# A decoder layer on one core: the rounding of the feed-forward rows moves from VectorE to ScalarE, and every engine's order is written anew

## The reference

```
x = layernorm(x + attention(x))        # width 256, 16 heads, windows of 128 positions
x = layernorm(x + ssm(ctx, z=x))       # state space: 512 channels, 16 states, 512 steps
x = layernorm(x + ffn(x))

def activation_quant(x):
    s = 127.0 / jnp.max(jnp.abs(x), axis=-1, keepdims=True)
    return jnp.clip(jnp.round(s * x), -128, 127) / s
xq = activation_quant(rms_norm(x))
g = jax.nn.silu(ternary_matmul(xq, W_g))
u = ternary_matmul(xq, W_u)
return ternary_matmul(g * u, W_d)      # the weights enter by their sign alone
```

## Time and profile before

| | |
|---|---|
| time, three runs | 989.22, 989.76 (median), 994.29 us |
| the profiled execution | 994.08 us, its span 992.4 us |
| mean TensorE clock granted in the span | 0.901 of full speed |
| busiest engines | DVE 865.3, PE 844.2, ACT 659.4, POOL 440.6 us |

### The profile page before, as it was taken

How to read it: one execution, slowest core, us unless ns; L and a number is a source line. 1 busy time by engine, 2 the same in 40 slices (tenths; PEclk the granted TensorE clock), 3 DMA queues, 4 the chain that set the end, 5 groups by cost and what they waited for, 6 DMA issues and landing times.

```text
span 992.4 us, 12690 instructions
## 1 busy us (share of the span) xinstructions
PE 844.2 (85%) x4258; PEld 532.1 (54%) x4258; DVE 865.3 (87%) x1200; ACT 659.4 (66%) x1115; POOL 440.6 (44%) x259
## 2 busy tenths in 40 slices
PE   1987887799978988999979889989978889876997
PEld 1446575585446565665446555665446565553453
DVE  0388999999799899999789999999789999999564
ACT  1586556566679586886687687886777687783332
POOL 2025755552335473542355564551365654554000
PEclk9997667769888889999998998999989999999899
DMA  7022323330100020100101121100000010000000
GB/s 221 31 77 76 106 96 129 95 97 11 44 11 33 22 75 22 37 18 12 44 12 33 33 75 29 36 11 12 23 13 31 33 41 25 32 13 11 11 12 32
DMA packets 29215, 43.92 MB, mean 44 GB/s; under 512 B 6128, under 2 KB 10096, under 8 KB 29152
## 3 DMA queue, kind: packets, MB, share of 16 engines
q1 hardware_dynamic: 25808, 41.74, 13.0%
q10 hardware_dynamic: 3344, 1.38, 0.6%
HBM read 38.78 MB, written 4.33 MB: 43 GB/s over the span
## 4 chain that ended last, share of the span: by engine, by line
DVE 45%; PE 29%; issue 15%; ACT 8%; POOL 2%; SPq 1%; DMA 1%; DVEq 0%; POOLq 0%; ACTq 0%
DVE h L1463 16%; DVE acc L1480 11%; PE bank_f L2355 3%; PE bank_a L2214 3%; PE bank_m L2331 3%; DVE s_pT L1348 2%; PE bank_f L2430 2%; DVE p_lo L1548 2%; ACT L896 2%; DVE g_p L1544 2%; DVE neg_max L1354 2%; PE bank_a L2259 2%; ACT d_a L861 2%; ACT L861 2%; PE bank_m L2297 2%
## 5 line engine op out<-in xcount | busy, mean ns | idle before, releaser
L514 POOL TENSOR_TENSOR b_x<-u,b_row 128x1024 f32<-128x1024 f32 x124 | 315.4, 2549 | 274.7 <-DVE h L1463 273.9
L1463 DVE TENSOR_TENSOR_SCAN h<-d_a,b_x 128x1024 f32<-128x1024 f32 x128 | 294.5, 2309 | 1.5 <-ACT d_a L861 1.5
L2331 PE MATMUL bank_m<-ident,h 128*128 128x128 f32 x1024 | 179.5, 309 | 51.6 <-DVE acc L1480 40.7
L861 ACT ACTIVATE d_a<-delta,a_neg 128x511 f32<-128x511 f32 x256 | 168.9, 712 | 33.1 <-DVE h L1463 32.7
L2331 PEld LDWEIGHTS bank_m<-ident,h 128*128 128x128 f32 x1024 | 134.6, 160 | 99.1 <-DVE h L1463 37.5
L1480 DVE SCALAR_TENSOR_TENSOR acc<-bank_m,c_cols,acc 128x512 f32<-128x512 f32 x256 | 185.8, 737 | 1.9 <-PE bank_m L2331 0.2
L896 ACT ACT_TABLE_LOAD x48 | 61.6, 1283 | 56.6 <-PE bank_f L2355 56.4
L791 ACT ACTIVATE s_pT<-s_pT,neg_max 128x128 f32<-128x128 f32 x256 | 81.4, 389 | 18.1 <-DVE neg_max L1354 18.0
L502 POOL TENSOR_TENSOR rs<-ve,neg_half 128x1 f32<-128x1 f32 (+1 forms) x36 | 36.3, 1009 | 120.1 <-DVE neg_mean L1565 69.0
L2241 PE MATMUL bank_a<-k_par,qT 32*128 32x256 f32 x256 | 79.6, 433 | 8.0 <-DVE s_pT L1348 6.1
L2259 PEld LDWEIGHTS bank_a<-v_aug,s_pT 128*128 128x128 f32 x512 | 70.8, 212 | 11.1 <-ACT s_pT L799 7.0
(11 more groups left out here) (180 smaller groups left out, 1476.7 us busy)
## 6 DMA issues: line engine op xcount, KB each, us to landing
b_row<-bc_rows SPq DMA_DIRECT2D x64, 256.0 KB, 3.1
x_next<-in_x_dram SPq DMA_DIRECT2D x4, 1024.0 KB, 5.5
y<-in_L_ffn_W_g_dram SPq DMA_DIRECT2D x16, 256.0 KB, 2.7
xn<-in_L_ffn_W_u_dram SPq DMA_DIRECT2D x16, 256.0 KB, 2.7
g_p<-in_L_ffn_W_d_dram SPq DMA_DIRECT2D x16, 256.0 KB, 3.0
out_dram<-y SPq DMA_DIRECT2D x16, 256.0 KB, 2.0
cx<-in_ctx_dram SPq DMA_DIRECT2D x4, 512.0 KB, 5.1
wc<-in_L_attn_Wc_dram SPq DMA_DIRECT2D x1, 512.0 KB, 10.0
```

The source lines that it names most:

```text
L514: nc.gpsimd.tensor_tensor(b_x[:, half], du[:, halves(half)], b_row[:, n % 2].unsqueeze(1).to_broadcast([P, EH, S]), ALU.mult)\
L861: last = nc.scalar.activation(d_a[:, half, c, 1:S], delta[:, half * EH + c, 1:S], ACT.Exp, scale=a_neg[:, half * EH + c, bass.ds(n, 1)])
L1463: nc.vector.tensor_tensor_scan(flat(h[:, (n + 1) % 2, halves(half)]), flat(d_a[:, half]), flat(b_x[:, half]), 0.0, ALU.mult, ALU.add).then ...
L2331: last = tr(bank_m[bank][:, c * P:(c + 1) * P], h[:, (n + 1) % 2, c, i * P:(i + 1) * P], ident[:])
```

## The change

1. `quantise` loses its last two instructions. ACT gets them as `round_rows`, two activations with the function Identity: the first adds `ROUND` (a column of the new tile `round_col`) to the row times `q_mul`, the second subtracts `ROUND` and writes 16 bits. PE's transposes wait for the new semaphore `xq_ready`.
2. The lower clip, which was part of the second rounding step, joins the upper one in DVE's copy of the transposes, in batches and in the tail.
3. The lists of all engines are written anew, in all their parts. `round_rows` is placed in ACT's lists.
4. In the tail `tail_product` waits for the transposes of two products before, since the buffer it writes is no longer covered by the order alone; and the second wait for the copied transposes is given to `tail_ups` too.

```diff
-Q_STEPS = 6
+Q_STEPS = 4
+        round_col = sb("round_col", [P, 2])
-        CONSTS = 10
+        CONSTS = 12
+            nc.gpsimd.memset(round_col[:, 0:1], ROUND).then_inc(consts_done, 1)
+            nc.gpsimd.memset(round_col[:, 1:2], -ROUND).then_inc(consts_done, 1)
...
+            def round_rows(n, t):
+
+                act.wait_ge(q_step, Q_STEPS * n + Q_STEPS)
+                nc.scalar.activation(xn[:], x2b[:, t], ACT.Identity, bias=round_col[:, 0:1], scale=q_mul[:, 0:1])\
+                    .then_inc(xn_ready, 1)
+                act.wait_ge(xn_ready, n + 1)
+                nc.scalar.activation(xq[:], xn[:], ACT.Identity, bias=round_col[:, 1:2]).then_inc(xq_ready, 1)
...
             def quantise(n, b, t):
...
-                dve.wait_ge(q_step, base + 4)
-                nc.vector.tensor_scalar(xn[:], rows, q_mul[:], ROUND, ALU.mult, ALU.add).then_inc(q_step, 1)
-                dve.wait_ge(q_step, base + 5)
-                nc.vector.tensor_scalar(xq[:], xn[:], -ROUND, Q_MIN, ALU.add, ALU.max).then_inc(q_step, 1)
             def quantised_T(n):
...
-                                        Q_MAX, None, ALU.min).then_inc(f_free[1], 1)
+                                        Q_MAX, Q_MIN, ALU.min, ALU.max).then_inc(f_free[1], 1)
...
             def tail_product(w, q):
                 k = NQ * w + q
+                if k >= 2:
+                    dve.wait_ge(tail_pT, k - 1)
...
             def quantised_T(n):
-                pe.wait_ge(q_step, Q_STEPS * n + Q_STEPS)
+                pe.wait_ge(xq_ready, n + 1)
...
-                quantise(row(b, w + 1), b - 1, w + 1)
...
+                quantise(row(b, w + 1), b - 1, w + 1)
                 low(row(b, w), 2)
```

1415 lines of the change are left out of this document (714 added, 701 removed).

## The result

The changed kernel takes 985.54 us (median of 7 runs, 983.44 to 986.33) against 991.8 us for the kernel before beside it: a ratio of 0.9928, with a 95% interval of 0.9901 to 0.9955. The forecast was 965.0 us, range 953 to 981. The direction was right; 6 us were won where 25 were forecast. The profiled execution took 985.54 us (span 983.8), against 994.1 before, so the two traces are 8.6 us apart.

The account below looks back on a forecast made before the run. DVE bounds inside batches, late PE and ACT work at seams and opening, PE in the tail. Terms -11.4 - 4 - 9 - 1 + 0.7 = -24.7 us, from median 989.76 to 965.0 us, range 953 to 981.

Parts of the forecast that it names:

- signs of being wrong: DVE's score waits growing over 5 us a seam, scans waiting 10 us or more for decays, transposes' copy over 0.5 us.
- signs of being right: DVE busy about 850 us, ACT 683, `relu`'s wait under 8, second and third seams 43 to 46, tiles 1 us shorter.
- Rounding leaves DVE: In batches and seams, two DVE instructions a row go, 0.95 us for each of 12 rows: 11.4 us saved.
- The copy, nothing: DVE's copy of the transposes gets a second operation at no cost; bounds nothing to 4.2 us more.
- ACT, hidden: ACT's two added instructions, about 1.5 us a row and 24 us in all, hide where ACT idles in batches and seams.
- The opening, -4 us: With `hidden` last on PE, `relu` starts 3.7 us earlier; 4 us saved, bounds 0 and 12.1.
- The seams, -4.5 each: Second and third seam: `relu`'s waits of 3.37 and 1.15 us go, 4.5 us a seam, 9.0 for two.
- the step as I described it: Second and third seam: both first `dt_projection` ahead of `hidden` on PE, so `relu` finds `magnitude` done; 4.5 us a seam.
- The first seam, -1: `hidden` stands ahead in both orders; only about 1 us of the waits for scores is addressed.
- rival 4: No change: seams and opening give nothing, half the rounding reappears as waits; about 984 to 995 us, chance 0.07.
- The tail's start, +0.7 us: At the tail's start the first row's rounding, slower on ACT, comes 0.6 us later plus a hand-over: 0.7 us lost.
- The base: The time the savings are taken from: median of three runs, 989.76 us, giving 965.0 us (-2.5%).

Follow-up runs that it names:

- opening_act: The changed kernel with `magnitude(0, 3)` and `exponential(0, 1)` ahead of `hidden(0, 0)` on ACT in the opening: 984.31 us, 0.992 of the kernel before.
- xT_apart: The changed kernel with `magnitude(0, 3)`, `exponential(0, 1)` ahead of `hidden(0, 0)` on ACT and batch 0's x transposes outside `delta`: 981.44 us, 0.9889 of the kernel before.
- best2: The changed kernel with old ending, `magnitude(0, 3)`, `exponential(0, 1)` before `hidden(0, 0)`, batch 0's x transposes outside `delta`, first seam's fourth gate before `queries(1, 0)`: 975.74 us.
- dt_first: Old orders, rounding on ACT behind each tile's last `probs_T`, plus second and third seams' `dt_projection`s (PE) and `magnitude`, `exponential` (ACT) before `hidden`: 990.15 us, 0.9984 of kernel before.

## Why the forecast was wrong

None of the signs of being wrong that the prediction named came up, and these signs of being right did (DVE 850.6 us busy, `relu`'s waits 7.3, scans 2.6, the copy 0.41): the forecast failed on waits that it did not list.

*Rounding leaves DVE, -11.4 us.* The mechanism was right, the size nearly: 8.8 us in the old orders with the pair well placed (0.9914). The decays behind it in the queue, to which I gave slack, waited: scans lost 5.3 us where the pair stood early. The rule of the Trainium skill, "ScalarE: Activation LUTs", section "Rules for kernel authors", that additions and multiplications belong on VectorE, did not hold for the time here: the pair costs 1.53 us there against 0.97, and moving it won 0.9%.

*The copy, nothing.* Right: 414 ns against 404. *ACT, hidden.* Right in the changed kernel (scans waited 2.6 us).

*The opening, -4 us: wrong, nothing that the stages tell.* The failing step is to take `relu`'s start 3.7 us earlier as the gain of the chain, with the scores as the only thing that `hidden`, now last, can delay. I priced `relu`'s wait and did not ask what the operation behind it waits for: the correction writes the tile that `hidden` reads, so with `hidden` last it waits for that instead (5.28 us in opening_act, none in xT_apart). The fourth `magnitude`, which I had seen fall behind, waited 5.77 us and not 3, since `hidden` stood ahead of it on ACT too and ran partly at the lower clock. With both waits removed the first stage took 111.2 to 112.1 us in three traces, 2.4 to 3.3 under the 114.5 of the kernel before, so most of the 4 us was there to be won.

*The seams, -4.5 each.* Without the rounding the stages gave -0.5 and -6.1, 6.6 of 9. The waits named did go; the same overlooked wait for `hidden` is 0.96 us there. In the second seam's stage stand 3.6 us of waits at stretches of the lower clock; without these (best2) it gave the forecast's 8.3. So the size was about right for the whole new order; the forecast had no term for the clock. That the step as I described it wins 4.5 us by itself is refuted by dt_first, which lost by it: what the seams gave came of the whole order there, and that its size is near the forecast's is luck.

*The first seam, -1.* The stage came out as forecast, -2.9, but it spreads by 10 us among kernels with the same lists, and it has a new wait of 6.17 us for a gate behind `queries` on ACT in it, so the agreement tells nothing.

*Inside batches and the ending: not a term at all.* I took the new lists to be neutral where I had found no wait to remove. They are not, and this is the other failing step: +5.7 us in the last stage where -1.2 was forecast. Three waits for `state_T`, 5.8 us together, stand in it, each behind a stretch at the lower clock; the kernel before has none there. The old ending gives 3 to 5 us back. The time is that of rival 4 (984 to 995), for which I had 0.07, but not by its mechanism, since the rounding did not reappear as waits.

*The tail's start, +0.7 us.* Right: from the last step of the variance to the first transposes 4.14 us (906.68 to 910.82) against 3.52, and from the first product to the end of the last 66.3 us against 66.0:

```profile
910.82 0.61 PE L2404 MATMUL bank_a<-ident_bf,xq 128*128 128x128 bf16 x4 [10.09 <-ACT xq L903]
911.95 1.89 PE L2431 MATMUL bank_f<-wuT,d_a 128*128 128x512 fp8e4 x4 [0.52 <-DVE d_a L1603]
...
977.17 1.03 PE L2452 MATMUL bank_f<-wdT,p_lo 128*128 128x512 f16 x4
```

*The base.* The forecast hung on the median of three runs, 989.76; the medians of later ones lay at 991.8 to 994.3, 2 us or more of the miss. *What stays open:* why the clock falls where it does, and so how much of the new orders' loss in the last stage (11.4 us without the move) belongs to the orders and how much to the stretches at the lower clock in it. No run here sets the clock by itself.
